# A transformer layer on one core: the first stage in three products of rounded fp32 parts, value rows in the same pass, late queries behind all keys

## The reference

```
xn  = layernorm(x)
q, k, v = xn @ Wq.T, xn @ Wk.T, xn @ Wv.T            # 16 heads of 16
attn = softmax(q k^T / 16) v                         # over all 4096 keys
scores = softmax(xn @ gate_w.T); top 2 of scores + gate_b over 8 experts
y = sum over the two: score * (silu((xn@w1+b1)*(xn@w3+b3)) @ w2 + b2)   # hidden size 352
z = the same expert form with shared weights, for all tokens
out = x + attn + y + z
```

## Time and profile before

| | us |
|---|---|
| median of 3 runs (lowest, highest) | 2172.42 (2171.32, 2177.13) |
| profiled execution's own time | 2174.9 |
| its span | 2172.7 |
| busy: TensorE, ScalarE, VectorE, GpSimd | 2146.7, 2009.4, 800.6, 246.7 |
| first product of scores starts | 114.89 |
| first exponential starts | 116.15 |
| mean granted clock of TensorE | 0.997 |

### The profile page before, as it was taken

How to read it: one execution, slowest core, us unless ns; L and a number is a source line. 1 busy time by engine, 2 the same in 40 slices (tenths; PEclk the granted TensorE clock), 3 DMA queues, 4 the chain that set the end, 5 groups by cost and what they waited for, 6 DMA issues and landing times.

```text
span 2172.7 us, 37941 instructions
## 1 busy us (share of the span) xinstructions
PE 2146.7 (99%) x15618; PEld 964.2 (44%) x15618; DVE 800.6 (37%) x1514; ACT 2009.4 (92%) x2209; POOL 246.7 (11%) x242
## 2 busy tenths in 40 slices
PE   8999999999999999999999999999999999999998
PEld 4632344444444444444444444444444444444322
DVE  6321143344344334334334434334334334544200
ACT  4599999999999999999999999999999999999998
POOL 0100465610000000000000000000000002223200
PEclk9999999999999999999999999999999999999999
DMA  7671334332222222213122222313213222332120
GB/s 245 212 283 33 94 120 128 99 90 65 62 78 63 76 56 79 78 54 85 53 72 70 76 64 70 79 50 82 75 51 89 64 71 73 104 99 64 56 78 3
DMA packets 223595, 187.24 MB, mean 86 GB/s; under 512 B 112039, under 2 KB 194558, under 8 KB 223166
## 3 DMA queue, kind: packets, MB, share of 16 engines
q1 hardware_dynamic: 211598, 149.41, 23.7%
q0 software_dynamic: 11824, 35.40, 5.0%
HBM read 130.21 MB, written 54.53 MB: 85 GB/s over the span
## 4 chain that ended last, share of the span: by engine, by line
PE 92%; ACT 7%; DVE 0%; DMA 0%; issue 0%; DVEq 0%
PE PS L658 41%; PE PS L645 29%; PE PS L670 12%; ACT probs L852 7%; PE PS L681 6%; PE PS L551 3%; PE PS L588 1%; PE PS L540 0%; PE PS L561 0%; DMA resid<-in_x 0%; DVE o_t L1151 0%; DVE stats L957 0%; ACT L852 0%; DVE probs L981 0%; ACT hid L843 0%
## 5 line engine op out<-in xcount | busy, mean ns | idle before, releaser
L852 ACT ACTIVATE probs<-PS 128x1024 f32<-128x1024 f32 x2048 | 1919.8, 1080 | 95.4 <-PE PS L645 80.7
L658 PE MATMUL PS<-probs,v_head 128*32 128x512 f32 x8192 | 1002.4, 601 | 1.3 <-ACT probs L852 1.0
L645 PE MATMUL PS<-q_ring,k_stack 50*128 50x512 f32 x4096 | 740.8, 446 | 6.9 <-ACT probs L852 6.2
L645 PEld LDWEIGHTS PS<-q_ring,k_stack 50*128 50x128 f32 x4096 | 332.6, 184 | 626.6 <-ACT probs L852 567.4
L658 PEld LDWEIGHTS PS<-probs,v_head 128*32 128x32 f32 x8192 | 206.6, 108 | 448.2 <-issue 358.5
L1176 DVE TENSOR_SCALAR gate_in<-PS,bias_sb 128x256 f32<-128x256 f32 x165 | 79.6, 482 | 754.7 <-PE PS L670 722.8
L670 PE MATMUL PS<-x_hi,w_hi 128*128 128x256 f32 (+1 forms) x660 | 201.3, 305 | 0.0
L670 PE MATMUL PS<-x_hi,w_lo 128*128 128x256 f32 (+1 forms) x660 | 186.5, 283 | 0.0
L670 PE MATMUL PS<-x_lo,w_hi 128*128 128x256 f32 (+1 forms) x660 | 185.6, 281 | 0.0
L907 POOL DMA_DIRECT2D slot_y<-y_sb x39 | 27.9, 716 | 1285.0 <-DVE y_sb L1244 1251.5
L670 PEld LDWEIGHTS PS<-x_hi,w_hi 128*128 128x128 f32 (+1 forms) x660 | 118.6, 180 | 60.0 <-issue 60.0
(11 more groups left out here) (132 smaller groups left out, 1092.5 us busy)
## 6 DMA issues: line engine op xcount, KB each, us to landing
w_raw<-in_w SPq DMA_DIRECT2D x110, 352.0 KB
k_stack<-qk_parts SPq DMA_DIRECT2D x120, 128.0 KB
w_raw<-in_w SPq DMA_DIRECT2D x55, 256.0 KB
q_ring<-qk_parts SPq DMA_DIRECT2D x384, 32.0 KB
slot_x<-part_a SPq DMA_DIRECT2D x39, 256.0 KB, 2.4
slot_in<-slot_x SPq DMA_DIRECT2D x156, 64.0 KB, 2.4
slot_y<-y_sb POOLq DMA_DIRECT2D x39, 256.0 KB, 2.5
k_stack<-qk_parts SPq DMA_DIRECT2D x136, 64.0 KB
```

Source lines behind the costliest of these rows:

```text
L645: last = pe.matmul(bank(2 * score_buffer(turn, g) + r), k_stack[rows, kt * P:(kt + 1) * P], q_ring[rows, sweep, i * QC:(i + 1) * QC], star ...
L658: last = pe.matmul(bank(O_BANK)[VW * j:VW * (j + 1), :], v_head[:, kt, :], probs[:, slot, (j % 2) * QC:(j % 2 + 1) * QC], start=(kt == 0), ...
L852: nc.scalar.activation(probs[:, prob_slot(g), :], bank(2 * score_buffer(h, g), 2), ACT.Exp, scale=ENERGY_SCALE).then_inc(s_exp, 1)
```

## The change

The transposed tokens are no longer kept in fp32 as operands. ScalarE takes each chunk's transposes twice (`take_tokens`), rounded to float32r into a ring of four chunks (`xh`) and in full into a double buffer (`xfull`); VectorE subtracts (`tokens_low`) and gives the rest, `xl`. Query, key, value and router weights are split the same way once, at the start: ScalarE rounds, VectorE subtracts. Each projection is then six products (high by high, low weights by high tokens, high weights by low tokens, for two halves of the features) in place of two fp32 ones, and a value pair twelve in place of four.

The value pairs 0 to 9 (tokens of the first five chunks) move into the chunk loop, in banks 0 and 1, which they share with the transposes. Keys of all eight chunks and queries of the first four are projected in the loop; the queries of chunks 4 to 7 come behind it, in banks 2 to 4, with the steps of the norm bound between them, then pairs 10 to 15. The norms of keys and queries have semaphores of their own, and the shift rows are made and stored in two halves of the tokens. Each chunk's full tokens are stored to DRAM from the double buffer in the loop. The stores of keys and of queries are now separate transfers. The buffers for the query parts are laid over the value buffer, the staging buffer and the normalised tokens. The load of the first shift rows moves ahead of the flag.

The diff, cut to the parts named here:

```diff
+FIRST = NCH // 2
+XRING = 4
+PAIRS = NT // 2
+LATE_PAIR = 10
+def key_job(c):
+    return 4 * c if c < FIRST else 4 * FIRST + DT * (c - FIRST)
+def query_job(c):
+    return 4 * c + DT if c < FIRST else 4 * FIRST + DT * c
+def pair_bank(n):
+    return 0 if n < LATE_PAIR else 2 * ((n - LATE_PAIR) % 3)
+def late_bank(m):
+    return 2 + m % 3
...
+            for c in range(NCH):                                    # SyncE
+                sp.wait_ge(s_xt, DT * (c + 1))
+                sp.dma_start(x_rows[:, :, c * QC:(c + 1) * QC], xfull[:, c % 2, :, :]).then_inc(s_xd[c % 2], 16)
+                store_keys(c)
                 if c:
+                    sp.wait_ge(s_kst[(c - 1) % 2], stored(c - 1))
                     load_k_chunk(c - 1)
+                if c < FIRST:
+                    store_queries(c)
+                if c == FIRST:
+                    for half in range(2):
+                        sp.wait_ge(s_qst[half], stored(FIRST - 2 + half))
                     load_q_rows(0, 0)
+            store_queries(4)
+            store_queries(5)
+            sp.wait_ge(s_kst[(NCH - 1) % 2], stored(NCH - 1))
             load_k_chunk(NCH - 1)
+            store_shift(0)
+            store_queries(6)
+            store_queries(7)
+            sp.wait_ge(s_sst, 16 * NP_)
+            load_q_shift(0, 0, s_q[0])
...
+            def project(c, w, i, b):                                # TensorE
...
+                for dt in range(DT):
+                    pe.wait_ge(s_xh, DT * c + dt + 1)
+                    pe.matmul(bank(b), wqk_hi[:, w, dt, cols], moving(hi, dt), start=(dt == 0), stop=False)
+                    pe.matmul(bank(b), wqk_lo[:, w, dt, cols], moving(hi, dt), start=False, stop=False)
+                pe.wait_ge(s_xl, c + 1)
+                for dt in range(DT):
+                    last = pe.matmul(bank(b), wqk_hi[:, w, dt, cols], moving(lo, dt), start=False, stop=(dt == DT - 1))
...
+            for c in range(FIRST):
+                keys(c, 0)
+                if c:
+                    value_rows(2 * c - 1)
+                turn_xn(c + 1)          # waits for the copy of the last value pair
+                keys(c, 1)
+                queries(c, 0)
+                key_norms(c)            # waits for both squares of the keys
+                queries(c, 1)
+                value_rows(2 * c)
+                query_norms(c)
+            for c in range(FIRST, NCH):
+                keys(c, 0)
+                if c + 3 < LATE_PAIR:
+                    value_rows(c + 3)
                 if c < NCH - 1:
                     turn_xn(c + 1)
+                keys(c, 1)
+                if c < NCH - 1:
+                    key_norms(c)
+            late_queries(4, 0)
+            key_norms(NCH - 1)
+            late_queries(4, 1)
+            late_queries(5, 0)
...
+            def take_tokens(c):                                     # ScalarE
                 act.wait_ge(s_tr, c + 1)
+                if c >= 2:
+                    act.wait_ge(s_xd[c % 2], 16 * (c // 2))
+                    act.wait_ge(s_xl, c - 1)
+                for dt in range(DT):
+                    nc.scalar.activation(xh[c % XRING][:, dt, :], bank(dt), ACT.Copy).then_inc(s_xh, 1)
+                    nc.scalar.activation(xfull[:, c % 2, dt, :], bank(dt), ACT.Copy).then_inc(s_xt, 1)
...
             root(0)
+            act.wait_ge(s_const, 16 * N_CONST)
+            nc.scalar.activation(wqk_hi[:, :, :, :], wqk, ACT.Copy).then_inc(s_wh, 1)
+            take_tokens(0)
             root(1)
+            act.wait_ge(s_const2, 16 * N_CONST2)
+            nc.scalar.activation(wvg_hi[:, :, :], wvg, ACT.Copy).then_inc(s_vwh, 1)
+            for c in range(FIRST):
+                split_keys(c, 0)
+                if c:
+                    keep_values(2 * c - 1)
+                take_tokens(c + 1)
+                if c == 0:
+                    root(2)
+                split_keys(c, 1)
+                split_queries(c, 0)
+                split_queries(c, 1)
+                keep_values(2 * c)
                 if c == 1:
                     root(3)
                 if c == 3:
                     root(4)
+            for c in range(FIRST, NCH):
+                split_keys(c, 0)
+                if c + 3 < LATE_PAIR:
+                    keep_values(c + 3)
+                if c < NCH - 1:
+                    take_tokens(c + 1)
+                split_keys(c, 1)
...
+            for c in range(FIRST):                                  # VectorE
+                key_rest(c, 0)
+                tokens_low(c + 1)
+                key_rest(c, 1)
+                if c % 2 == 0:
+                    deviations(c // 2 + 2)
+                normalise(c + 2)
+                query_rest(c, 0)
+                query_rest(c, 1)
                 if c in (1, 3):
                     variances(c // 2 + 3)
+            for c in range(FIRST, NCH):
+                key_rest(c, 0)
+                if c < NCH - 1:
+                    tokens_low(c + 1)
+                if c == FIRST:
+                    deviations(4)
+                if c < NCH - 2:
+                    normalise(c + 2)
+                key_rest(c, 1)
```

More of the change, by code:

```diff
@@ L408, in _ @@
             sp.wait_ge(s_flag, 1)
             flag = sp.value_load(flag_i[0:1, 0:1], min_val=0, max_val=1)
+            store_shift(1)
+            for half in range(2):
+                sp.wait_ge(s_qst[half], stored(NCH - 2 + half))
             with sp.If(flag):
@@ L490, in next_keys @@
                 load_k_rows(h + 1, i)
+            for half in range(2):
+                sp.wait_ge(s_xd[half], 16 * FIRST)
             load_up(0)
@@ L555, in norms @@
-            def norms(c):
-                pe.wait_ge(s_sq, c * NJ + NJ)
-                own = slice(P - H - H * c, 2 * P - H - H * c)
-                for w in range(2):
-                    for dt in range(DT):
-                        last = pe.matmul(bank(6 + w), hones_b[:, dt, own], sq[:, c % 2, w * DT + dt, :],
-                                         start=(c == 0 and dt == 0), stop=(c == NCH - 1 and dt == DT - 1))
-                last.then_inc(s_nr, 1)
+                turned[0] += 1
@@ L565, in _ @@
             turn_xn(0)
             pe.wait_ge(s_hb, 2)
[L567 to L570, removed]
+            pe.wait_ge(s_wl, 1)
+            for c in range(FIRST):
[9 more added lines that the diff above has]
+                query_norms(c)
@@ L789, in root @@
                 nc.scalar.activation(ln_t[:, 1, lo:hi], ln_t[:, 0, lo:hi], ACT.Sqrt).then_inc(s_std, 1)
-            def take_xn(c):
+            def take_tokens(c):
                 act.wait_ge(s_tr, c + 1)
[L794 to L804, removed]
+                if c >= 2:
+                    act.wait_ge(s_xd[c % 2], 16 * (c // 2))
+                    act.wait_ge(s_xl, c - 1)
+                for dt in range(DT):
+                    nc.scalar.activation(xh[c % XRING][:, dt, :], bank(dt), ACT.Copy).then_inc(s_xh, 1)
+                    nc.scalar.activation(xfull[:, c % 2, dt, :], bank(dt), ACT.Copy).then_inc(s_xt, 1)
@@ L908, in store_y @@
                                     y_sb[:, u % 2, :].rearrange("p (t d) -> p t d", t=TPU)).then_inc(s_yst[u % 2], 16)
-            pool.wait_ge(s_xd, 16)
+            for half in range(2):
+                pool.wait_ge(s_xd[half], 16 * FIRST)
             load_shared(0)
@@ L1039, in _ @@
                 dve.wait_ge(s_tr, NCH)
-                dve.wait_ge(s_nr, NCH)
+                dve.wait_ge(s_nk, NCH)
+                dve.wait_ge(s_kst[1], stored(NCH - 1))
+                for half in range(2):
+                    dve.wait_ge(s_qst[half], stored(NCH - 2 + half))
                 V.memset(q_every[SHIFT:SHIFT + NP_, :].bitcast(f32), 0.0).then_inc(s_qzero, 1)
@@ L1268, in _ @@
             add_output(0)
-            dve.wait_ge(s_xd, 16)
+            for half in range(2):
+                dve.wait_ge(s_xd[half], 16 * FIRST)
             up_hi(0)
```

328 lines of the change are left out of this document (217 added, 111 removed).

## The result

The changed kernel takes 2189.19 us (median of 4, 2188.31 to 2191.31) where the kernel before takes 2173.41 beside it: a ratio of 1.0071, 95% interval 1.0059 to 1.0084, so 15.8 us slower. The forecast was 2183.6, range 2173 to 2195. The profiled execution took 2188.59 for a span of 2186.8. The result lies in the range, just above the 2189 at which the likeliest case ends. All ratios leave out one execution of e8_fill, of 2855.4 us at a mean granted clock of 0.655.

A forecast was written before the change was run, and what follows sets the result against it. TensorE's chain was taken as the bound, 92% of the span. Attention starting at 123.0 instead of 114.9 gave 8.2 us, plus 3 for the clock: 11.2 us on the median 2172.4, so 2183.6, range 2173 to 2195.

The forecast's parts named there:

- the likeliest case: Waits and the token store outweigh the saved products: 2183.6 us, by its own terms 2178 to 2189; chance 0.53.
- The products: TensorE's projections at six products, 1.29 us, and value pairs at twelve, 1.45 us: 19 us less if TensorE never waits.
- The chunks: First-stage loop: 11.2 us per chunk for chunks 1 to 3, 8.03 for chunks 4 to 6, including waits for ScalarE.
- the copy of the pair: In each chunk, transposes wait for ScalarE to copy the value pair sharing their banks: 0.17 + 0.61 + 0.02 us.
- the squares: In each chunk, key norms wait for ScalarE's token copies and second key half's copy and square, startable at 7.60 us.
- The two root waits: ScalarE's square roots after chunks 1 and 3 wait for VectorE's variances, making the pair's copy 1.95 us late, twice.
- The token store of chunk 5: Chunk 7's token copies wait 4.7 us for this store, issued behind key and query loads; bounds 0 and 9 us.
- Pair 12's store: Before attention, the copy of pair 12 waits for the store of query parts it overwrites: 0.7 us, between 0 and 3.
- The clock: TensorE's idle time in chunk 0 and before chunk 7 slows the products that follow: 3 us counted of 7.
- rival C: Short waits hold the clock down, doubling TensorE's part in chunks 4 to 6: attention at 137, 2194.6 us; chance 0.24.
- Rival B: No wait for the token store and a warm clock: attention at 117.6, total 2175.1 us; chance 0.17.
- D: Buffers are loose enough and TensorE stays the bound in the first stage: 15.4 us less, 2157.0 us; chance 0.06.

The follow-up runs named there:

- e8_fill: The changed kernel with products nobody reads put into TensorE's waits before the key norms of chunks 0 and 4 to 6: ratio 1.0055 to the kernel before.
- e2: The changed kernel with each chunk's value pair moved behind the transposes and the next projection, same work: ratio 1.0028 to the kernel before.
- e10: e7_all with the first query loads behind the first shift rows' store, plus two extra products per projection: ratio 1.0013 to the kernel before.
- e5_q6: The changed kernel with chunk 6's query parts in the token copy buffer, so pair 12 waits only for chunk 4's query store: ratio 1.0048 to the kernel before.
- e7_all: The changed kernel with later roots, moved value pairs, a separate value-weight semaphore, moved query parts and earlier shift rows: ratio 0.9987 to the kernel before.
- e4_pad: The changed kernel with two extra products at the start of every projection, putting back TensorE work: ratio 1.0089 to the kernel before.

## Why the prediction was right, point by point

**The mechanism.** Rightly told: TensorE's time saved, and given back in the waits. The e2 and e10 results show it from both sides: e2_pairs gains 9.3 us with no work taken away, and the padding costs 9.8 us only once the waits are gone.

**The products.** Predicted 0.215 us at 512 columns and 0.121 at 264. On the timeline of TensorE in the changed kernel, from start to start:

```profile
102.60 0.39 PE L636 MATMUL PS<-x_parts,wqk_lo 128*128 128x512 f32 x1
102.83 0.40 PE L635 MATMUL PS<-x_parts,wqk_hi 128*128 128x512 f32 x1
...
115.53 0.28 PE L697 MATMUL PS<-wvg_hi,x_parts 128*128 128x264 f32 x1
115.65 0.28 PE L698 MATMUL PS<-wvg_lo,x_parts 128*128 128x264 f32 x1
```

0.233 and 0.122 over the six-product groups. I took the bf16 norm products as the nearest row for the wide ones; the 256-column products of the same kind, scaled (0.118 x 2 = 0.236), would have been right. A projection is 1.40 and not 1.29.

**The chunks.** First key splits of chunks 1, 3, 5, 6 were due at 30.6, 54.9, 76.1, 84.2 (a projection and the hand-over behind the starts that the forecast gives), and stand at 32.25, 58.48, 80.35, 88.81. Chunk 1 is late by the clock, the next by 0.11 per projection and another spell at half clock (0.79 over 48 to 56). The period of chunks 5 to 6 is 8.46 against 8.03. The two waits inside it were forecast at 0.8 for the copy of the pair and 1.9 for the squares (the walk's 7.60 less 4.41 and 1.29), and the trace has 0.79 and 1.75:

```profile
82.49 1.07 PE L621 MATMUL PS<-ident_sb,probs 128*128 128x128 f32 x8 [0.79 <-ACT v_all L977]
...
86.69 0.61 PE L665 MATMUL PS<-probs,hones_b 128*128 128x512 bf16 x2 [1.75 <-ACT probs L954]
```

The two root waits are 3.3 us on ScalarE each.

**The token store of chunk 5.** Predicted wait 4.7, bounds 0 to 9; 1.5 in the changed kernel (and none in the trace of e5_q6). The key loads took 2.5 us and not 3.9, the landing 2.9 and not 4.5. In e7_all, where the chunks before it are quicker, it is 3.5: the term depends on who is early.

**Pair 12's store.** This is the term that was mis-sized: 0.7, "between 0 and 3", measured 5.2. The forecast places this store behind the last key load and the shift rows but gives no landing time for it, and no working for the 0.7. The store took 8.9 us to land. Stretches of 2 us of the changed kernel (granted clock, DMA share, GB/s at the end):

```profile
110.00:112.00 2.00, 2.00 (x10) 1.52 (x10) 0.59 (x2) 1.08 (x2) 0.00 (x0) 1.00 1.04 400
...
114.00:116.00 2.00, 2.00 (x13) 1.77 (x12) 0.69 (x1) 1.72 (x4) 0.00 (x0) 1.00 0.25 74
116.00:118.00 2.00, 2.00 (x15) 1.46 (x14) 0.69 (x1) 1.61 (x3) 0.00 (x0) 1.00 0.72 233
118.00:120.00 2.00, 1.95 (x17) 1.73 (x17) 1.82 (x4) 0.66 (x2) 0.00 (x0) 1.00 0.97 350
```

The queries of four chunks, 4 MB, now leave in the last 18 us, beside key loads, and the transfers run at up to 400 GB/s there. The forecast speaks of the issues in front of the store and not of the bytes beside it. That the bytes are the cause is argued and not shown: the queue had run down to 74 GB/s when this store was issued (115.87), and what went beside it was mostly chunk 7's megabyte, issued right behind. Before, a chunk's queries left with its keys.

**The clock.** Counted at 3 us. It fell in chunk 0 and in chunk 7 as supposed, and in chunk 2, where it was not: 10.2 us at half in this trace, at most 5.1 us of delay. Nor does the column for the granted clock tell everything: from 19.02 to 21.58, where it reads 1.00, products of 512 columns start 0.43 us apart, just as they do at 0.50 from 26.75 to 28.03. The first projections of the kernel before, which the forecast calls cold, are such a case: 5.97 us for eight records, with the column at 1.00. That it varies from execution to execution was not foreseen. The part of the Trainium skill cited there ("TensorE: Matmul & The Clock Gate", "A second HAM failure mode: psum-queue depth-cycling") has the idle times swing the clock. The trace has both levels in one stage, but chunks 5 and 6, with idle times of 1.75 and 0.79 us in each 8.5, ran at the full clock, so rival C's doubling there didn't come.

**The sum.** 123.0 and 3 gave 126.0 for attention; it was 127.8: 4.5 more for pair 12 and some 3 for the wide products, less 3.2 for the token store. These come to 130.3; the 2.5 us between that and 127.8 were not taken apart (some of the products' 3 fall into waits, as in e4_pad). So the forecast is as near as it is partly by luck: its two large misses, the token store and pair 12, have opposite signs. (123.0 less 114.9 is 8.1 and not 8.2, which moves the forecast by 0.1.) Another 1 us came inside attention (half clock at its start) and 1.7 between the medians and the profiled executions.

Rival B falls with the waits that are there, D with the chain. C is wrong in chunks 4 to 6, where it put most of its cost; the spells at half clock that it also had in chunk 0 and around chunk 7 did come.

## What to carry to other kernels

Cutting an engine's work is worth only what the written order lets through: walk one period of the loop through every wait, and if a cheaper operation makes another engine's queue the end of it, move the work that doesn't depend on that queue into the gap before counting on the gain. Here the same work in another order, with two waits cut down to what they need and one buffer moved, turned 0.71% slower into 0.32% faster. Ahead of a deadline don't take a landing time for granted (8.9 us here, where the quickest store of queries landed in 2.8), and ask of each wait on a counted semaphore whether a later transfer than the one needed is counted in; and when one such wait is taken away, look what lands next, since two of them often end together.

## What the runs showed of the hardware

Products of float32r with 128 rows have an interval of 0.118, 0.122 and 0.233 us at 256, 264 and 512 columns, the bf16 norm products 0.215 at 512: 8% more for the same columns. The cause wasn't tried. And the fall of TensorE's clock in a stage with short waits is not the same from one execution to the next: with the same instructions up to there, granted 0.63 over 24 to 28 us in one, after 2.53 us idle, and 1.00 in another, after 3.20 us idle.
